# Attention on one core: four key slots of every pair's first unit turned through memory and by VectorE, and strided transposes that alternate with value matmuls

## What is computed

```python
hn  = group_norm(x, gn1_scale, gn1_bias)            # 8 batches, 512 channels, n = 1024 positions
qkv = einsum('bchw,oc->bohw', hn, w_qkv) + b_qkv    # 8 heads, ch = 64 channels each
wgt = softmax(einsum('bct,bcs->bts', q * ch**-.25, k * ch**-.25), axis=-1)
a   = einsum('bts,bcs->bct', wgt, v)
out = x + group_norm(einsum('bchw,oc->bohw', a, w_proj) + b_proj, gn2_scale, gn2_bias)
```

## Time and profile before

| what | value |
|---|---|
| median of 3 runs | 3376.01 us (3374.05 to 3376.51) |
| the profiled execution | 3375.88 us, its span 3373.7 us |
| TensorE busy | 3351.2 us, 99% |
| VectorE, ScalarE, GpSimd busy | 63%, 55%, 32% |
| granted TensorE clock | 1.00 of full speed over the whole span |

### The profile page before, as it was taken

One profiled execution on the slowest core, in us unless ns is written; L12 is line 12 of the kernel. 1 busy time (PEld: TensorE's weight loads), 2 busy tenths in 40 slices (PEclk: granted clock), 3 DMA queues, 4 the chain that ended last, 5 costly groups with the idle time before them and its releaser, 6 DMA issues.

```text
span 3373.7 us, 51950 instructions
## 1 busy us (share of the span) xinstructions
PE 3351.2 (99%) x16816; PEld 2777.5 (82%) x16816; DVE 2132.7 (63%) x3489; ACT 1838.7 (55%) x3094; POOL 1064.3 (32%) x947
## 2 busy tenths in 40 slices
PE   8999999999999999999999999999999999999999
PEld 6888888888888888888888888888888888888887
DVE  5677357773578745786457854578555784557844
ACT  4677227862378523784337842388333882347822
POOL 1344104441045410453104531145211452124511
PEclk9999999999999999999999999999999999999999
DMA  8522244313534125331253212442224422343212
GB/s 340 149 67 59 79 131 124 93 34 94 140 99 101 62 57 151 103 86 76 53 167 91 73 75 76 144 101 63 93 61 144 98 63 94 92 139 70 63 57 75
DMA packets 109871, 332.15 MB, mean 98 GB/s; under 512 B 21760, under 2 KB 54784, under 8 KB 98816
## 3 DMA queue, kind: packets, MB, share of 16 engines
q1 hardware_dynamic: 107648, 322.15, 33.3%
q10 hardware_dynamic: 1920, 6.29, 0.9%
HBM read 162.68 MB, written 31.49 MB: 58 GB/s over the span
## 4 chain that ended last, share of the span: by engine, by line
PE 94%; DMA 2%; issue 1%; DVE 1%; SPq 1%; ACT 1%; POOL 0%; POOLq 0%; DVEq 0%
PE big L514 25%; PE big L648 14%; PE ops L634 14%; PE tps L619 14%; PE big L746 7%; PE big L655 5%; PE tps L819 5%; PE ops L819 5%; PE ops L598 3%; DMA ST<-ST 2%; PE tps L746 1%; SPq L419 0%; PE ops L746 0%; SPq L484 0%; PE ops L788 0%
## 5 line engine op out<-in xcount | busy, mean ns | idle before, releaser
L1097 POOL TENSOR_SCALAR PB<-PB,small 128x1024 f32<-128x1024 f32 x576 | 648.7, 1127 | 1294.8 <-DVE small L1342 1277.2
L1347 DVE TENSOR_TENSOR PT<-tps,PT 128x512 fp32r<-128x512 f32 x1024 | 652.5, 679 | 42.1 <-ACT PT L954 41.7
L1336 DVE TENSOR_REDUCE small<-big 128x1 f32<-128x1024 f32 x512 | 625.2, 1221 | 85.1 <-PE big L648 81.8
L954 ACT ACTIVATE PT<-tps 128x512 fp32r<-128x512 f32 x1024 | 564.1, 597 | 158.3 <-PE tps L619 155.4
L948 ACT ACTIVATE PB<-big,small 128x1024 f32<-128x1024 f32 x512 | 572.8, 1119 | 94.8 <-DVE small L1336 91.8
L634 PE MATMUL ops<-PT,VT 128*128 128x512 f32 x2048 | 599.1, 414 | 0.0
L648 PE MATMUL big<-ST 128*128 128x512 f32 x2048 | 554.2, 392 | 3.5 <-DMA ST<-ST 3.5
L619 PEld LDWEIGHTS tps<-ident,PB 128*128 128x128 f32 x4096 | 470.2, 140 | 95.4 <-DVE PT L1347 30.9
L619 PE MATMUL tps<-ident,PB 128*128 128x128 f32 x4096 | 545.7, 274 | 0.9
L648 PEld LDWEIGHTS big<-ST 128*128 128x128 f32 x2048 | 382.6, 188 | 91.5 <-issue 6.1
L634 PEld LDWEIGHTS ops<-PT,VT 128*128 128x128 f32 x2048 | 346.1, 189 | 47.1 <-DVE PT L1347 5.0
(11 more groups left out here) (188 smaller groups left out, 4911.7 us busy)
## 6 DMA issues: line engine op xcount, KB each, us to landing
ST<-ST SPq DMA_DIRECT2D x360, 256.0 KB, 5.3
W<-d_qk SPq DMA_DIRECT2D x32, 1024.0 KB, 7.0
W<-PB SPq DMA_DIRECT2D x256, 128.0 KB, 2.4
X<-in_x SPq DMA_DIRECT2D x8, 2048.0 KB, 10.2
W<-d_wp SPq DMA_DIRECT2D x8, 2048.0 KB, 11.9
W<-d_g SPq DMA_DIRECT2D x8, 2048.0 KB, 11.8
W<-d_m SPq DMA_DIRECT2D x8, 2048.0 KB, 7.7
W<-d_u SPq DMA_DIRECT2D x8, 2048.0 KB, 13.2
```

Source lines behind the costliest of these rows:

```text
L954: act_fn(pt_slot(u, s)[:, 0, :], tps[n % 2][:], ACT.Copy).then_inc(s_pt_hi, 1)
L1097: nc.gpsimd.tensor_scalar(PB[:, i, :], PB[:, i, :], rinv[:, i:i + 1], 1.0, ALU.mult, ALU.mult)\
L1336: V.tensor_reduce(negmax[:, i:i + 1], tile(("s", 4 * u + tb))[:], axis=AX.X, op=ALU.max, negate=True).then_inc(s_row_max, 1)
L1347: V.tensor_tensor(pt_slot(u, s)[:, 1, :], tps[n % 2][:], pt_slot(u, s)[:, 0, :].bitcast(f32), ALU.subtract).then_inc(s_pt_ready, 1)
```

## The change

Of the first unit of each of the first three pairs (`MOVED`: units 0, 4, 8), slots 4 to 7 leave the transpose path. When the unit's rows are scaled, SyncE stores columns 512 to 1023 of the four `PB` tiles to DRAM (`d_e`) and reads them back in quarters of 32 partitions into the first half of `X` (`F0`). VectorE turns four squares of 32x32 blocks from there into the second half of `X` (`square`), ScalarE copies the high part (`moved_hi`), GpSimd makes the low part (`moved_lo`), and TensorE's value matmuls for that unit come at steps 7 to 10 of each 16 (`MOVED_VALUES`). So that the stored rows are whole pieces of 128 columns, the second half of the keys of these three pairs is stored in another order (`keys_by_turn`): key (s, q, r) at column (q, r, s). For the units that still use TensorE in these pairs, slots 4 to 7 are then read with a step of four elements (16 bytes), and in those steps each two transposes are followed by one value matmul (`by_turns`). Projections move from steps 9 and 11 to 8 and 10, in another order of parts. `X` is loaded after the last low part of unit 8, and scaled at steps 50 to 56.

```diff
-QK_STEPS = (5, 7, 9, 11)
+QK_STEPS = (5, 7, 8, 10)
+MOVED = [4 * pair for pair in range(PAIRS - 1)]
+MOVED_SLOTS = [8 * u + s for u in MOVED for s in range(4, NT)]
+def transposed(step):
+    n = 2 * (step - LAG)
+    return [m for m in (n, n + 1) if m >= 0 and m not in MOVED_SLOTS]
+def by_turns(step):
+    strided = [m for m in transposed(step) if m % 8 >= 4 and m // 32 * 4 in MOVED]
+    return len(strided) == 2 and len(valued(step)) == 2
+SQUARES_FIRST, SQUARES_LAST = {7: (4, 5)}, {7: (6, 7)}
+MOVED_HI = {7: (4, 5), 8: (6, 7)}
+MOVED_LO = {6: (4, 5), 7: (6, 7)}
+MOVED_VALUES = {7: (0, 1), 8: (2, 3), 9: (4, 5), 10: (6, 7)}
-X_SCALE_STEPS = (20, 23, 26, 29)
+X_SCALE_STEPS = (50, 52, 54, 56)
...
+            def move_quarters(b, u):
...
+                for t in range(KB):
+                    sp.wait_ge(s_p_norm, b * 72 + 4 * u + t + 1)
+                    own_wait(sp)
+                    sp.dma_start(d_e[t], PB[:, t, HALF:N]).then_inc(s_moved_out[t // 2], 16)
+                for part in range(2):
+                    sp.wait_ge(s_moved_out[part], (b * len(MOVED) + MOVED.index(u) + 1) * 32)
+                    own_wait(sp)
+                    for q in range(QUARTERS):
+                        sp.dma_start(F0[32 * q:32 * q + 32, 2 * part:2 * part + 2, :],
+                                     d_e[2 * part:2 * part + 2].rearrange("t (q p) n -> p (t q) n", p=32)
+                                     [:, :, P * q:P * q + P]).then_inc(s_moved, 16)
...
-                    for t in range(4):
-                        last = nc.tensor.transpose(tps[n % 2][:, P * t:P * t + P],
-                                                   PB[:, 4 * (u % 2) + t, P * s:P * s + P], ident[:])
+                    for t in tiles:
+                        row = PB[:, 4 * (u % 2) + t, :]
+                        if s >= 4 and u // 4 * 4 in MOVED:
+                            keys = row[:, HALF:N].rearrange("p (k s) -> p s k", s=4)[:, s - 4, :]
+                        else:
+                            keys = row[:, P * s:P * s + P]
+                        last = nc.tensor.transpose(tps[n % 2][:, P * t:P * t + P], keys, ident[:])
...
+                    if by_turns(step):
+                        for m, v in zip(transposed(step), valued(step)):
+                            for i in range(2):
+                                transposes(m // 8, m % 8, range(2 * i, 2 * i + 2))
+                                values0(v, range(i, i + 1))
+                        continue
...
+                def moved_hi(n):
+                    act.wait_ge(s_squared, squared_count(b, n))
+                    act.wait_ge(s_values_read, b * len(MOVED_SLOTS) + MOVED_SLOTS.index(n) + 1)
+                    act_fn(pt_slot(n // 8, n % 8)[:, 0, :], squared(n % 8), ACT.Copy).then_inc(s_moved_hi, 1)
...
+                def moved_lo(n):
+                    pool.wait_ge(s_moved_hi, squared_count(b, n))
+                    slot = pt_slot(n // 8, n % 8)
+                    nc.gpsimd.tensor_tensor(slot[:, 1, :], squared(n % 8), slot[:, 0, :].bitcast(f32), ALU.subtract)\
+                      .then_inc(s_moved_lo, 1)
...
                 for n in range(4 * UNITS0):
                     normalise(n)
+                    for m in of_moved(n, MOVED_LO):
+                        moved_lo(m)
...
+                def square(n):
+                    u, s = n // 8, n % 8
+                    if s == 4:
+                        dve.wait_ge(s_moved, (b * len(MOVED) + MOVED.index(u) + 1) * 32 * QUARTERS)
+                    V.transpose(squared(s).rearrange("p (t q r) -> p t q r", t=KB, q=QUARTERS),
+                                F0.rearrange("p t (q r s) -> p s t q r", q=QUARTERS, s=4)[:, s - 4, :, :, :])\
+                     .then_inc(s_squared, 1)
```

More of the change, by code:

```diff
@@ L46, in qk_part, with of_moved, valued, qk_what @@
     return None
+MOVED = [4 * pair for pair in range(PAIRS - 1)]
+MOVED_SLOTS = [8 * u + s for u in MOVED for s in range(4, NT)]
+def of_moved(step, table):
+    unit = 4 * (step // 16)
+    return [8 * unit + s for s in table.get(step % 16, ())] if unit in MOVED else []
+def transposed(step):
+    n = 2 * (step - LAG)
+    return [m for m in (n, n + 1) if m >= 0 and m not in MOVED_SLOTS]
+def valued(step):
+    n = 2 * (step - LAG) - 2
+    return [m for m in (n, n + 1) if m >= 0 and m // 8 not in MOVED]
+def by_turns(step):
[5 more added lines that the diff above has]
+MOVED_VALUES = {7: (0, 1), 8: (2, 3), 9: (4, 5), 10: (6, 7)}
+def qk_what(j):
+    first, then = ((1, 1), (1, 0)), ((0, 1), (0, 0))
+    order = first + then if j < 4 else first[1:] + then + first[:1]
+    return (j // 4,) + order[j % 4]
 def a_parts(step):
@@ L233, in build @@
         s_ld_u = sem("ld_u")
+        s_moved_out = [sem(f"moved_out{i}") for i in range(2)]
+        s_moved = sem("moved")
+        s_squared = sem("squared")
+        s_moved_hi = sem("moved_hi")
+        s_moved_lo = sem("moved_lo")
+        s_values_read = sem("values_read")
         s_stack_a = sem("stack_a")
@@ L603, in project_qk @@
                 def project_qk(j):
-                    pair, what, half = j // 4, j % 4 // 2, j % 2
+                    pair, what, half = qk_what(j)
                     if j % 4 == 0:
@@ L631, in values0 @@
                         pe.wait_ge(s_v_ready, b * 6 + 6)
[L632 to L633 removed]
+                    if n in MOVED_SLOTS:
+                        pe.wait_ge(s_moved_lo, squared_count(b, n))
+                    else:
+                        pe.wait_ge(s_pt_ready, pt_count(b, n))
+                    for part in parts:
                         last = mm(ops[u % 2][:], VT[:, s, P * (u // 2):P * (u // 2) + P], pt_slot(u, s)[:, part, :],
                                   start=(s == 0 and part == 0), stop=(s == 7 and part == 1))
[L636 removed]
+                    if n + 4 in MOVED_SLOTS and parts[-1] == 1:
+                        last.then_inc(s_values_read, 1)
+                    if s == 7 and parts[-1] == 1:
                         last.then_inc(s_o_full, 1)
@@ L947, in exps @@
                     i = 4 * (u % 2) + tb
+                    if u - 2 in MOVED and tb == 0:
+                        for part in range(2):
+                            act.wait_ge(s_moved_out[part], (b * len(MOVED) + MOVED.index(u - 2) + 1) * 32)
                     act_fn(PB[:, i, :], t[:], ACT.Exp, bias=negmax[:, i:i + 1], accum_out=rowsum[:, i:i + 1])\
@@ L990, in body @@
                         qk_hi(qk_part(step))
[L991 to L994, removed]
+                    for m in of_moved(step, MOVED_HI):
+                        moved_hi(m)
+                    for m in transposed(step):
+                        pt_hi(m // 8, m % 8)
+                    if tb == 2 and u >= 2 and u - 2 not in MOVED:
+                        corr(u - 2, 0)
+                    if tb == 3 and u - 2 in MOVED:
                         corr(u - 2, 0)
@@ L1355, in body @@
                     u, tb, n = step // 4, step % 4, 2 * (step - LAG)
+                    for m in of_moved(step, SQUARES_FIRST):
+                        square(m)
                     if qk_part(step) is not None:
@@ L1365, in body @@
                         recip((step - 1) // 4, (step - 1) % 4)
-                    if n >= 0:
-                        pt_lo(n // 8, n % 8)
-                        pt_lo(n // 8, n % 8 + 1)
+                    for m in of_moved(step, SQUARES_LAST):
+                        square(m)
+                    for m in transposed(step):
+                        pt_lo(m // 8, m % 8)
                     if last_values(step) == NT - 1:
```

77 lines of the change are left out of this document (54 added, 23 removed).

## The result

The changed kernel takes **3389.78 us** (median of 6 runs, 3387.53 to 3390.52) against 3375.78 us for the kernel before on the same chip: a ratio of 1.0041 (95% interval 1.0029 to 1.0052). It is slower by 14 us. The forecast was 3360 us, faster. The profiled execution took 3389.99 us, its span is 3388.2 us.

What follows compares the result with a forecast made beforehand. The prediction took TensorE's summed work to bound the kernel, with VectorE and ScalarE close behind. From 3375.88 us, -41.5 - 3 + 18.4 + 10 = -16.1 gave 3360 us, range 3333 to 3397.

Steps and rivals of the forecast that it cites:

- Term 1: Steps 7 and 8 of a pair: 384 transposes removed at 108 ns, -41.5 us, and short waits for VectorE, -3 us.
- term 3: Hand-over at steps 7 to 10: late qk_lo behind squares, +5 us, and late GpSimd normalise, +5 us; +10 in all.
- Term 2: Plain steps with turns: four of eight strided transpose loads exposed, 32 ns more for each of 576, +18.4 us.
- rival A: Strided TensorE loads are free, 3341 us, chance 0.24; its sign: starts within a pair of transposes stand 108 ns apart.
- B: Strided TensorE loads go at half the pace, 18 steps per batch, 62 us more, 3403 us, chance 0.20.
- rival C: VectorE bounds step 7: squares read with gaps take twice 693 ns and delay qk_lo, 3393 us, chance 0.10.
- Rival D: Steps 7 to 10: TensorE merely waits for the longer path, freed time unused, 3376 us, chance 0.08.
- the two signs: A plain step with turns longer than 2.95 us; TensorE idle around steps 7 to 10 above 1.7 us per moved unit.
- Parts at nothing: Late X load, scale_x on GpSimd (0.45 us to spare at step 50), key writes with gaps, extra DMA: no cost.

Runs made afterwards that it cites:

- the square above: Changed kernel with turns: step of four 3389.8 us, loads in a row 3383.0; without turns: 3366.4 and 3357.5 us.

## Why the prediction was wrong

**Term 1 (transposes removed, -41.5 and -3 us)** was right in kind, and in size as far as the steps tell. Steps 6 to 10 shrank by 3.53 us per batch, 28 us, while TensorE had 5.18 us less to do there; the missing 1.65 us per batch are its new waits in steps 7 and 9, net of old ones that went. The pace of 108 ns, and not the record of 274, was the right price: by the record, 384 transposes would be 105 us. By the pace, and with the 20 us found for term 3 below, these steps should give -24.5 us; they gave -28, so some 4 us are not accounted for.

**Term 2 (strided loads, +18.4 us)** was priced too high: in a row the strided transposes start 120 ns apart and not 108, so 12 ns more, not 32, and the step of four costs 6 to 10 us in the square above. With turns the second transpose of a pair starts 108 ns behind the first, with the step or without it (medians of the turned steps 15, 16 and 19 in the changed kernel and in the one with loads without gaps). That is what the prediction had named as rival A's sign. The load that was to cost 32 ns keeps the pace, and two transposes and a value together take 467 ns instead of 453. Rivals A (0 us) and B (62) were both off; of the two A was nearer. The Trainium skill ("SBUF — State Buffer", Door 1: The DMA port swizzle) says that an access to a new 16-byte line pays unless the line is hit at least twice. The runs agree that it pays, and add how much: 11% of the pace of transposes in a row, 58% for VectorE's square. The same paragraph also gives 4 fp32 as how far a stride is free; at that step of four the runs show 120 ns against 108 and 1078 against 682, so it is not free here.

**Term 3 (hand-over, +10 us)** named the right places: `qk_lo` late behind two squares at step 7 of the first pair, and step 9. It gave the first 0.6 us and it was 1.3: the squares take 1078 ns and not the 693 of the earlier trace rows, 0.8 us for two, and with short squares 0.5 us of loss were left (5.10 against 4.59 us). This is rival C's cause, smaller than its doubling and in one pair of three. It gave the second 0.2 us and the three pairs lose 0.4; that GpSimd's low parts hold it is shown for the first pair alone. Together some 20 us instead of 10.

**The step that failed** is the rule on which the sum rests, "what is taken from TensorE is taken from the time, unless another engine is pushed past it", with the words "its own load is contiguous, as before" as all that was said of the turns, and nothing at all of `corr`, which the diff moves by one step. For a plain step with turns I added up TensorE's own work, 2.85 us, and the turned steps took 2.77 to 2.80: that sum was right to 0.1 us. What I did not follow is when each slot is done. With ScalarE 89% busy and VectorE 91%, the chain from a slot's transposes over the high part, the exponential, the reciprocal, the row maximum and the low part back to the next transposes has little slack. The turns lengthen it by half a microsecond, the late `corr` by another 0.6, and TensorE pays at the next step that needs the result: 23 us for the first, 20 us for the second, 30 us for both (3389.8 to 3359.6). Alone each costs less, 10.5 and 6.8 us: part of one delay fits in the slack, both do not. Each has a single-edit run against it; none was among my rivals. Rival D had a longer path that TensorE waits for, but at steps 7 to 10, where most of it was covered.

With what was measured in the place of each term, -44.5 + 8 (step of four) + 20 (hand-over) + 30 (turns and `corr`) is +13.5 us, against the 14 of the result. Neither of the two signs that I had named for being wrong came: no plain step with turns passed 2.95 us, and steps 7 to 10 lost 1.7 us in the first pair, just at the bound, and 0.4 in the others. The loss stood at step 13, where no sign looked.

**"Parts at nothing"** holds without the turns, where moving the scaling of `X` gave 2 us, within the spread. In the changed kernel steps 54 and 57 lost 0.58 us per batch, and most of it went with the turns. The 0.45 us to spare that the prediction counted at step 50 were gone at step 57, where the `normalise` behind the scaling ended last.

Without the turns and with `corr` in its old place the kernel takes 3359.6 us. The forecast of 3360 meets that number, but by errors that cancel (the loads 10 us too dear, the hand-over 10 us too cheap), and it was not a forecast of this kernel. It is luck too that 3389.8 us lies in the stated range, next to rival C's 3393: the gaps in the squares, which C rests on, cost 7 us of the 33 that C gives them.

## What to carry to other kernels

When an edit reorders work on the engine that sets the pace, its own sum is half of the reckoning: follow also when each product is finished, and who stands behind it on the engines that are 90% busy. A line that is moved "where there is room" must be checked on the engine whose in-order queue it joins: the same `corr` cost 4 us in one kernel and 20 in another, and squares moved behind the instruction that they blocked in one pair cost 34 us instead of giving 10. Undo every part of a bundle on its own; here most of a bundle's gain was hidden by two of its lines, and the bundle without them is 0.5% faster than the kernel before, and 0.8% with `last_v_lo` a step later and the scaling at other steps.

## What the runs showed of the hardware that was not expected

The price of a step of four fp32 elements in SBUF depends on who reads. VectorE's 128x512 transpose went from 682 to 1078 ns. TensorE's load of 128 columns ahead of a transpose has a record of 198 ns in the mean with turns and 207 in a row instead of 140, but the pace of transposes in a row only went from 108 to 120 ns. The record grew by 67 ns and the pace by 12, so most of the longer load still runs beside other work of TensorE.
